# Gate copies out of PSUM and the high part of the second FFN's activations on VectorE instead of ScalarE, from the fifth tile on

## The reference

```python
xn = layernorm(x)
x = x + attn0(xn) + ffn0(xn)      # attn0: causal, 32 query heads of 8, 8 key/value heads, RoPE, biases
xn = layernorm(x)                 # ffn0: e4m3 inputs and weights, gelu_tanh(xn@W0) * (xn@W1) -> e4m3 -> @W2, bf16 results
x = x + attn1(xn) + ffn1(xn)      # attn1: RoPE, scores over the 16 heads of one token (b s h t), wo
# ffn1: ternary weights (scale and sign per 64), h = silu(gate) * up, h * rsqrt(mean(h^2) + eps), @Wproj
```

## Time and profile before

| what | us |
|---|---|
| median of three runs | 625.43 |
| lowest, highest | 624.88, 625.59 |
| the profiled execution | 626.23 |
| its span | 624.5 |
| TensorE matmul busy in it | 570.9 (91%) |
| ScalarE busy | 488.0 (78%) |
| VectorE busy | 441.5 (71%) |
| GpSimd busy | 268.6 (43%) |

### The profile page before, as it was taken

One profiled execution on the slowest core, in us unless ns is written; L12 is line 12 of the kernel. 1 busy time (PEld: TensorE's weight loads), 2 busy tenths in 40 slices (PEclk: granted clock), 3 DMA queues, 4 the chain that ended last, 5 costly groups with the idle time before them and its releaser, 6 DMA issues. The chain is left out here.

```text
span 624.5 us, 13580 instructions
## 1 busy us (share of the span) xinstructions
PE 570.9 (91%) x5085; PEld 291.6 (47%) x5085; DVE 441.5 (71%) x903; ACT 488.0 (78%) x925; POOL 268.6 (43%) x380
## 2 busy tenths in 40 slices
PE   3697899989999999999999999999999999998882
PEld 1333434425455545555453445555444452555661
DVE  6899789878597667867887676665565553577563
ACT  2488899978988998999987897979998988844330
POOL 4776566364334228613985563253152410613000
PEclk9799899989999999999999999999999999999997
DMA  8801101030404030221301004440504004044540
GB/s 285 296 2 35 31 5 34 2 51 2 69 17 62 27 52 1 41 39 18 52 1 36 1 1 68 60 65 6 86 2 69 8 2 68 27 78 85 85 53 30
DMA packets 150920, 30.45 MB, mean 49 GB/s; under 512 B 133952, under 2 KB 149568, under 8 KB 150848
## 3 DMA queue, kind: packets, MB, share of 16 engines
q1 hardware_dynamic: 150272, 29.19, 23.5%
q10 hardware_dynamic: 576, 0.33, 0.2%
HBM read 19.02 MB, written 10.49 MB: 47 GB/s over the span
## 5 line engine op out<-in xcount | busy, mean ns | idle before, releaser
L904 ACT ACTIVATE Pt<-psS 128x512 f32<-128x512 f32 x576 | 299.0, 622 | 33.2 <-PE psS L655 28.1
L669 PE MATMUL psV<-Pt,vaug 128*32 128x512 f32 x1152 | 150.1, 608 | 3.2 <-POOL Pt L1539 2.9
L1539 POOL TENSOR_SCALAR_AFFINE_SELECT Pt<-Pt 128x512 f32<-128x512 f32 x128 | 90.9, 746 | 62.0 <-ACT Pt L904 61.9
L655 PE MATMUL psS<-qTf,kTf 32*128 32x512 f16 x576 | 73.6, 387 | 5.2 <-DVE kTf L1158 1.9
L655 PEld LDWEIGHTS psS<-qTf,kTf 32*128 32x128 f16 x576 | 20.0, 91 | 83.2 <-ACT Pt L904 46.9
L1594 POOL TENSOR_TENSOR ss<-ss,mhalf 128x1 f32<-128x1 f32 x16 | 9.0, 565 | 93.7 <-DVE ss L1383 93.7
L669 PEld LDWEIGHTS psV<-Pt,vaug 128*32 128x32 f32 x1152 | 25.4, 108 | 46.8 <-issue 30.4
L954 ACT ACTIVATE stage<-psS 128x512 f32<-128x512 f32 x64 | 33.1, 606 | 10.6 <-PE psS L772 10.5
L1585 POOL TENSOR_TENSOR r<-qk,cos 128x256 f32<-128x256 f32 x16 | 14.5, 904 | 50.6 <-ACT qk L938 49.2
L1389 DVE SCALAR_TENSOR_TENSOR qtmp<-qtmp,ss 128x1024 f16<-128x1024 f32 x16 | 22.1, 1378 | 13.3 <-ACT qtmp L974 13.2
L1520 POOL TENSOR_TENSOR rt<-qkv,cs 128x320 f32<-128x320 f32 x16 | 16.6, 1035 | 33.8 <-DVE qkv L1119 26.1
(11 more groups left out here) (351 smaller groups left out, 1262.9 us busy)
## 6 DMA issues: line engine op xcount, KB each, us to landing
qkvscr<-rqkv SPq DMA_DIRECT2D x16, 384.0 KB, 2.7
G<-qkvscr SPq DMA_DIRECT2D x48, 128.0 KB, 3.7
stage<-in_wg SPq DMA_DIRECT2D x4, 512.0 KB, 7.2
oscr<-o SPq DMA_DIRECT2D x16, 128.0 KB, 3.0
at<-oscr SPq DMA_DIRECT2D x16, 128.0 KB, 2.1
out<-yout SPq DMA_DIRECT2D x16, 128.0 KB, 3.0
x<-in_x SPq DMA_DIRECT2D x1, 1536.0 KB, 12.0
r<-in_wgu SPq DMA_DIRECT2D x2, 512.0 KB, 7.3
```

The source lines that it names most:

```text
L655: e.matmul(psS[j][:], kd[32 * j:32 * j + k, h, 128 * at:128 * at + 128], qd[32 * j:32 * j + k, 4 * h:4 * h + 4, :].rearrange("p s n -> p ( ...
L669: ins = e.matmul(psV[32 * j:32 * j + 32, :], vaug[:, at, j, 32 * h:32 * h + 32], Pt[(4 * Q + j) % NP][:], start=(kb == 0 and h == 0), stop ...
L904: e.activation(Pt[u % NP][:], psS[j][:], ACT.Exp, scale=SC0 / UP / UP).then_inc(S["exp"], 1)
L1539: e.affine_select(out=p, in_=p, pattern=[[0, 4], [1, 128]], compare_op=ALU.is_ge, fill=0.0, base=0, channel_multiplier=-1).then_inc(S["mas ...
```

## The change

The gate copies of halves 8 to 31 (tiles 4 to 15) become a VectorE stage `gd`, and the high part of tiles 4 to 15 a VectorE stage `hxd`. Tiles 0 to 3 keep `g` and `hxa` on ScalarE. Waits and the emptying of `up`'s bank follow the new stage. All five strings of `ORDER` are new.

```diff
+BY_DVE = 4
+def gate_copied(m):
+    n = m // 2
+    return ("gd", m + 1 - 2 * BY_DVE) if BY_DVE <= n < NT else ("g", m + 1 - (2 * (NT - BY_DVE) if n >= NT else 0))
+def high_made(n):
+    return ("hxd", n + 1 - BY_DVE) if BY_DVE <= n < NT else ("hxa", n + 1 - (NT - BY_DVE if n >= NT else 0))
...
-    "wo0": lambda n: ("xa", n + 1), "up": lambda m: ("fh" if m % 2 else "g", m // 2 + 1), "down": lambda n: ("yff", n + 1),
+    "wo0": lambda n: ("xa", n + 1), "up": lambda m: ("fh", m // 2 + 1) if m % 2 else gate_copied(m // 2), "down": lambda n: ("yff", n + 1),
...
             def hxT(m):
                 n, pt = divmod(m, 2)
-                w.wait_ge("hx" if pt else "hxa", n + 1)
+                w.wait_ge(*(("hx", n + 1) if pt else high_made(n)))
...
             def sq(m):
                 half = m % 2
-                w.wait_ge("g", m + 1)
+                w.wait_ge(*gate_copied(m))
...
+            def gd(m):
+                bank = psM[filled["up", 2 * m] % len(psM)]
+                w.wait_ge("up", 2 * m + 1)
+                w.wait_ge("sq", m - 1)
+                w.wait_ge("a8c", m - 1)
+                e.tensor_copy(gb[:, m % 2, :], bank[:]).then_inc(S["gd"], 1)
+
+            def hxd(n):
+                w.wait_ge("rsg", n + 1)
+                w.wait_ge("ssq", n + 1)
+                e.tensor_scalar(hx_b[:, 0, :], h1, ss[n % len(ss)][:, 2:3], None, ALU.mult).then_inc(S["hxd"], 1)
...
             def hx(n):
                 sn = ss[n % len(ss)]
-                w.wait_ge("hxa", n + 1)
+                w.wait_ge(*high_made(n))
```

Of the new strings, the starts and ends that the prediction speaks of (old, then new):

```diff
 "dve", start
-vz.0 ln0.0 xn.0 ln0.1 xnTc.0 ln0.2 idc.0 xn.1 ln0.3 xn.2 qkvc.0 tsc.0 va.0 xnTc.1 tsc.1 wide.0 w8.0 xnTc.2
+ln0.0 vz.0 xn.0 idc.0 ln0.1 xnTc.0 ln0.2 xn.1 ln0.3 xn.2 qkvc.0 xnTc.1 tsc.0 wide.0 w8.0 tsc.1 va.0 w8.1
 "pe", start
-xnT.0 qkv.0 ts.0 ts.1 xnT.1 qkv.1 xnT.2 qxT.0 qxT.1 qkv.2 qk.0 qk.1 xnT.3 up.0 qxT.2 qxT.3 td.0 pv.0 up.1
+xnT.0 qkv.0 xnT.1 ts.0 qkv.1 ts.1 xnT.2 qxT.0 qxT.1 qkv.2 xnT.3 up.0 qk.0 qxT.2 qxT.3 qk.1 up.1 td.0 up.2
 "dve", end
-o1r.15 ssm.15 o1.15 yo.14 hx.15 yout.14 hTc.30 hTc.31 at1Tc.15 yo.15 yout.15
+o1r.15 ssm.15 at1Tc.14 o1.15 hxd.15 hx.15 yo.14 hTc.30 yout.14 hTc.31 at1Tc.15 yo.15 yout.15
```

More of the change, by code:

```diff
@@ L195 @@
 }
-PARTS = {"qxT": 2, "fxT": 3, "fTc": 3, "mT": 2, "up": 4, "qkv1": 2, "gT": 2, "gu": 4, "hxT": 2, "sq": 2, "fh": 2, "th": 2,
+PARTS = {"gd": 2, "qxT": 2, "fxT": 3, "fTc": 3, "mT": 2, "up": 4, "qkv1": 2, "gT": 2, "gu": 4, "hxT": 2, "sq": 2, "fh": 2, "th": 2,
          "tg": 2, "mTc": 2, "g": 2, "ge1": 2, "ge3": 2, "sg": 2,
@@ L218, in one_round @@
             stage, part = (word + ":0").split(":")[:2]
+            if stage in ("g", "hxa") and BY_DVE <= n < NT or stage in ("gd", "hxd") and not BY_DVE <= n < NT:
+                continue
             steps.append((stage, PARTS.get(stage, 1) * n + int(part)))
@@ L268 @@
 idc vz tab cst w8 w8m w8s tsc tm tcs tw ln0 xn xnTc qkvc va wide q0 kl kTc qTc fTc rmax rcomb mxn mTc ob att attTc xa ge1 ge3 ge3b a8c yff
-ln1 xn1 xn1Tc v1c ro1 ro2 gTq m1 gTm o1r o1 sg hh ssm hx hTc at1Tc yo yout ysum flag
+ln1 xn1 xn1Tc v1c ro1 ro2 gTq m1 gTm o1r o1 sg hh ssm hx hTc at1Tc yo yout ysum gd hxd flag
 zero gz zf rs0 rope ql mask ge4 xf rs1 xl ro1p rsg w8a""".split()
@@ L1450, in out_of_range @@
                 e.tensor_copy(flag[0:1, 0:1], hl1[0:1, 0:1]).then_inc(S["flag"], 1)
-            run = {"idc": idc, "vz": vz, "tab": tab, "cst": cst, "w8": w8, "w8m": w8m, "w8s": w8s, "tsc": tsc, "tm": tm, "tcs": tcs,
+            run = {"gd": gd, "hxd": hxd, "idc": idc, "vz": vz, "tab": tab, "cst": cst, "w8": w8, "w8m": w8m, "w8s": w8s, "tsc": tsc, "tm": tm, "tcs": tcs,
                    "tw": tw, "ln0": ln0, "xn": xn, "xnTc": xnTc, "qkvc": qkvc, "va": va, "wide": wide, "q0": q0, "kl": kl, "kTc": kTc,
```

## The result

The changed kernel takes **629.98 us** (median of 18 runs, 628.42 to 631.26) against 625.22 us (18 runs of the kernel before beside it): ratio 1.0068, 95% interval 1.0053 to 1.0083, so 4.3 us slower. The forecast was 623.9 us. A second set of 6 runs of the same code gave 628.82 us, ratio 1.0045 [1.0009, 1.0082]. The time lies beside that of the rival "shared banks come free later" (629.7 us), but the experiments show another mechanism than the one priced there.

A forecast was written before the change was run, and what follows sets the result against it. TensorE, busy 453.05 of 462 us in the body, was taken as the bound. Terms -2.3 + 0.5 - 0.4 + 0.7 = -1.5 us turn a median of 625.43 into 623.9 us, range 619.5 to 629.0.

The forecast's parts named there:

- shared banks come free later: Rival: gate banks freed later by VectorE, 0.24 us at each of 24 copies, +5.8; chance 0.31, including a worse order.
- The body's relief, -2.3 us: 100 to 562 us: ScalarE loses 18.7% of its non-exp work, so TensorE's 12.5 us of stretched qk shrinks by that share.
- The body's load on VectorE, +0.5 us: 100 to 562 us: 5.4 us of TensorE's 8.95 us idle time grows with VectorE's load, by 8.4%.
- TensorE's largest waits are all on VectorE: Body: the largest waits named in TensorE's matmul queue, 1.5, 1.3 and 1.1 us, were read as all on VectorE.
- Head, -0.4 us: First tiles: new strings reorder the memset, `idc`, `ts` and `up`; -0.4 us, bounds -2 and +2.
- My criterion: Prediction wrong if TensorE's lost time in the first 100 us, 24.56 us, moves by over 2 us.
- Tail, +0.7 us: Last tile: `hxd.15` behind `o1` on VectorE delays `dn1.15` and all after it; +0.7 us, bounds 0 and +2.5.
- The gate copy, 0.681 forecast: Price on VectorE of one 128x512 float32 gate copy from PSUM: 0.681 us, 24 of them 16.3 us.
- my step by 256 elements: High part's VectorE price: 0.408 us plus 3 x 0.262 us per 256 elements, from PSUM copies, gives 1.19 us.
- an estimate of 0.68 us: High part's lower price by the skill's two results per cycle: 4.6 us less VectorE body time, tail term 0.2.

The follow-up runs named there:

- e5: Kernel before, its strings kept; ScalarE's gate copies and high parts of tiles 4 to 15 cut in width, nothing added to VectorE: 624.61 us, ratio 0.9993.
- e1: Strings of the kernel before, with the 24 gate copies and 12 high parts both moved to VectorE: 631.00 us, ratio 1.0078.
- e9: Changed kernel, with VectorE's moved gate copies and high parts both cut to 8 columns: 628.21 us, ratio 1.0051.
- e16: All steps on ScalarE; the changed kernel's strings up to 138 us, then those of the kernel before: 626.58 us, ratio 1.0032.
- e6: Kernel before, ScalarE unchanged, plus 24 dummy VectorE sums where moved gate copies would stand: 630.79 us, ratio 1.0099.
- e3: Strings of the kernel before, with only the 24 gate copies moved to VectorE: 629.62 us, ratio 1.0057.
- e4: Strings of the kernel before, with only the 12 high parts moved to VectorE: 627.62 us, ratio 1.003.
- e7: Strings of the kernel before, gate copies moved to VectorE except those of tiles 5, 6, 9, 12 and 13: 625.72 us, ratio 1.0011.
- e18: The kernel before run and profiled again, not a line different: 624.99 us, ratio 0.9997.
- e17: The changed kernel run and profiled again, not a line different: 628.82 us, ratio 1.0045 to the kernel before.

## Why the prediction was wrong, by its steps

**The body's relief, -2.3 us: it did not come.** It took the share of ScalarE's work that goes and let the stretched qk shrink by that share. In the old strings this is roughly borne out: e5 takes 20.5 us off ScalarE and gains 1.3 us in the body, which makes an estimate of 1.8 us for the whole relief, and qk's busy time falls to 59.58 us in e5 and 59.45 in e1 (60.93 and 60.22 before). In the changed kernel qk is stretched by 2.8 us more, with VectorE's part cut as well (e9). What failed here is a step taken as given and never priced: that the rewritten strings leave the body's losses alone. Part of what the body loses more is only work drawn into the head (e16: -4.1 there, +4.0 in the body).

**The body's load on VectorE, +0.5 us: the step that failed.** I let 60% of TensorE's idle time grow by 8.4%. A load is not paid by averages. By that rule e6's 18.0 us are worth 0.3 us (an estimate: 18.0/320.05 of 5.4); they cost 4.0. With both sides in, the gate copies cost 2.9 net (e3), the high parts 1.5 (e4), both 4.6 (e1, body 45.8 to 50.4), where the prediction's two body terms together say -1.8. That is what turned the sign in the old strings. In the changed kernel the new strings' own placing brings VectorE's time down to 1.6 (e9 against the changed kernel), still three times the term. The rival "later banks" had the sign and, by chance, the size; its price, 0.24 us at each of 24 copies, is wrong: most copies cost nothing (e7), and a few cost 0.3 to 1.0 us each by what stands behind them.

The term also rested on a reading that is not right. The prediction says that TensorE's largest waits are all on VectorE. The longest in total is on GpSimd's mask, a row that stands above the three of the earlier trace rows in the same view:

```profile
PE psV L669 <- POOL Pt L1539: 2.0, 2, 1.2
```

A slip of less weight: the 60.93 us of the earlier trace rows are of 500 matmul records, 125 quads, so that qk's floor is 48.0 us and the stretching 12.9, not 12.5.

**Head, -0.4 us.** Not separable from chance: identical code moves by 1.4 us there (e18). What looked like a gain of 4 us is work drawn forward (e16). My criterion, the lost time of the first 100 us moving by over 2 us, was of no use: it went from 24.56 to 22.65 us in the changed kernel, and the kernel before, run again, shows 26.1.

**Tail, +0.7 us.** Measured +2.9 us in length in the first profile (60.6 to 63.5 us), +1.4 in the second. In the old strings the high parts cost 0.8 us (e1, e4), near the term by luck: 0.2 us of it is at the last tile, where the term was reckoned, the rest in front of it, where the prediction counted nothing. In the new strings the mechanism was to be `hxd.15` behind `o1`, as forecast, and it stands there:

```profile
609.89 0.42 DVE L1391 TENSOR_TENSOR o<-psC,rec 128x256 f32<-128x256 f32 x1
610.24 0.74 DVE L1273 TENSOR_SCALAR qtmp<-qtmp,ss 128x1024 f16<-128x1024 f32 x1
611.01 1.28 DVE L1419 SCALAR_TENSOR_TENSOR qtmp<-qtmp,ss 128x1024 f16<-128x1024 f32 x1
```

But from `pv.143` to `dn1.15` e9, where it is cut, and e17 take 58.3 us both. So `hxd.15` costs nothing there, and the +1.4 us is the order's: 0.4 us is the work of `o1T.11`, which the new string has behind `pv.143` and no longer ahead of it, and 1.0 is lost time. The other 1.4 in the first profile is the clock.

**Prices.** The gate copy, 0.681 forecast, took 0.683 to 0.686. The high part took 0.837 us in the mean (0.724 at least), not 1.19: my step by 256 elements, from copies out of PSUM, does not hold between two operands in SBUF. The Trainium skill, "VectorE: DVE Perf Modes" (Mode 2x_2P), by whose two results per cycle the prediction had an estimate of 0.68 us, was much nearer; the trace of the changed kernel agrees with it within 7% at the fastest and 23% in the mean. It did not matter: by that estimate the forecast would have been lower still, and farther off.

**The sum.** From the kernel before to the changed one, in lost time (means of the two profiles each, 112.7 and 117.05, a difference of 4.35 us; ratio 1.0068 is 4.3 us): VectorE's time in the body 1.6, the tail's order 1.0, the clock's fall in one of two profiles 0.7. The remaining 1.05 us is what the strings lose in head and body together with the steps cut (99.9 against a mean of 98.6, 1.3 us); it is no larger than the head's own variation, so that it is not shown. The relief, worth 1.3 us and more in the old strings, is inside these numbers and does not show as a gain. Why the new strings stretch qk was not taken apart place by place, and stays open. Nor did a version beat both kernels: the nearest, e5 and e7, can't be told from the kernel before.

## What to carry to other kernels

Where TensorE is busy all the time and its work is a fixed list, don't price a moved step by busy shares: go to each place where it will stand, and see which step is behind it in the new engine's queue and whether TensorE waits for that step's bank; ten of 24 copies cost all in the old strings, the rest nothing. Price both sides by themselves first, with a kernel that only takes the work away and one that only adds it: 1.3 us (for some 70% of the relief) against 4.0 for the gate copies' load would have warned of this change. When an order is written anew beside a change, the order is a change of its own, and part of a gain in one stretch may be work drawn from the next: compare sums of lost time, and run identical code twice before reading a microsecond.

## What the runs showed of the hardware

- TensorE's granted clock can fall from 1.00 to 0.50 for 2 to 3 us in the tail, in one profile of a program and not in the next (592 to 596 us, with 1.4 us lost), with the same instructions in the same order.
- From 138 us on, identical code repeats within 0.2 us in 415 us, while its first 138 us vary by 1.4. There the granted clock differs between runs, though that this is the cause is not shown (0.86 and 0.87 from 26 to 50 us, 0.97 and 1.00 from 50 to 100 us in the two profiles of the kernel before).
- A float32 `tensor_scalar` with a scalar by partition, SBUF to SBUF, 128x1024 to float16, took 724 to 1118 ns, median 749: 0.73 ns an element, where a quarter of the width took 408 ns, 1.6 ns an element.
